# Who issues the loads, and in what order: four adapters on one core, with ScalarE issuing the later weights

## The reference

```python
# itok_B_1_2: 4 expert numbers, here 1 or 2; x: (4, 512, 512); W_down: (3, 512, 256); W_up: (3, 256, 512)
Wd = W_down[stream]
bd = b_down[stream]
Wu = W_up[stream]
bu = b_up[stream]
g = ln_w[stream]
b = ln_b[stream]
residual = hidden_states
h = jnp.einsum('bsh,bhk->bsk', hidden_states, Wd) + bd[:, None, :]
h = jax.nn.gelu(h, approximate=False)
h = jnp.einsum('bsk,bkh->bsh', h, Wu) + bu[:, None, :]
h = residual + h
mean = jnp.mean(h, axis=-1, keepdims=True)
var = jnp.mean(jnp.square(h - mean), axis=-1, keepdims=True)
h = (h - mean) * jax.lax.rsqrt(var + LN_EPS)
return h * g[:, None, :] + b[:, None, :]
```

## Time and profile before

| | |
|---|---|
| median of the runs shown | 71.18 us (72.03, 70.78, 71.18) |
| the profiled execution | 71.47 us |
| its span (first to last instruction) | 69.5 us |
| TensorE busy | 57.6 us, 83% of the span |
| VectorE, GpSimd, ScalarE busy | 48.4, 39.6, 34.5 us |
| read from device memory, written | 10.50 MB, 4.19 MB |

### The profile page before, as it was taken

How to read it: one execution, slowest core, us unless ns; L and a number is a source line. 1 busy time by engine, 2 the same in 40 slices (tenths; PEclk the granted TensorE clock), 3 DMA queues, 4 the chain that set the end, 5 groups by cost and what they waited for, 6 DMA issues and landing times. The chain is left out here.

```text
span 69.5 us, 957 instructions
## 1 busy us (share of the span) xinstructions
PE 57.6 (83%) x290; PEld 46.9 (67%) x290; DVE 48.4 (70%) x95; ACT 34.5 (50%) x51; POOL 39.6 (57%) x43
## 2 busy tenths in 40 slices
PE   1980089999999999999999999999999999993000
PEld 1960043468978888888888888888899988880000
DVE  0079510503277999964999999369999989999920
ACT  0420049257999982469996073998035404030000
POOL 4000006002939999999997599999929503029300
PEclk9999999999999999999999999999999999999995
DMA  0699998499999999999910006620000166300551
GB/s 0 217 251 271 308 421 335 71 409 306 325 417 422 419 412 414 411 408 415 379 42 0 0 5 261 257 90 0 0 9 0 73 250 280 139 12 0 194 207 51
DMA packets 4756, 14.75 MB, mean 212 GB/s; under 512 B 528, under 2 KB 528, under 8 KB 4752
## 3 DMA queue, kind: packets, MB, share of 16 engines
q1 hardware_dynamic: 4176, 13.65, 51.5%
q10 hardware_dynamic: 576, 1.05, 5.1%
HBM read 10.50 MB, written 4.19 MB: 211 GB/s over the span
## 5 line engine op out<-in xcount | busy, mean ns | idle before, releaser
L536 PE MATMUL y_ps<-wu_hi,hid_hi 128*128 128x512 f32 x32 | 13.4, 418 | 0.0
L226 POOL TENSOR_TENSOR wu_lo<-w_raw,wu_hi 128x512 fp32r<-128x512 f32 x8 | 10.2, 1288 | 5.3 <-ACT wu_hi L282 5.3
L366 DVE BATCH_NORM_STATS2 stats<-y_ps 128x6 f32<-128x512 f32 x16 | 10.8, 689 | 3.0 <-PE y_ps L542 3.0
L215 POOL TENSOR_TENSOR x_lo<-x_raw,x_hi 128x512 fp32r<-128x512 f32 x10 | 12.7, 1292 | 0.0
L542 PE MATMUL y_ps<-wu_hi,hid_lo 128*128 128x512 f32 x32 | 12.6, 394 | 0.0
L538 PE MATMUL y_ps<-wu_lo,hid_hi 128*128 128x512 f32 x32 | 12.5, 392 | 0.0
L231 POOL TENSOR_TENSOR rstd<-var_eps,minus_half 128x2 f32<-128x2 f32 (+1 forms) x10 | 6.4, 637 | 9.9 <-DVE var_eps L374 9.9
L383 DVE SCALAR_TENSOR_TENSOR y_ps<-y_ps,mean_var,ln_gb 128x512 f32<-128x512 f32 x16 | 11.5, 749 | 0.0
L393 DVE SCALAR_TENSOR_TENSOR result<-y_ps,rstd,ln_gb 128x512 f32<-128x512 f32 x15 | 10.8, 743 | 0.3
L293 ACT ACTIVATE x_res<-x_raw,w_raw 128x512 f32<-128x512 f32 x16 | 10.2, 712 | 0.0
L449 PE MATMUL hid_ps<-x_raw,w_raw 128*128 128x512 f32 x8 | 5.7, 874 | 4.0 <-DMA w_raw<-weights 4.0
(11 more groups left out here) (35 smaller groups left out, 90.6 us busy)
## 6 DMA issues: line engine op xcount, KB each, us to landing
x_raw<-x_cols SPq DMA_DIRECT2D x6, 512.0 KB, 8.3
out<-result SPq DMA_DIRECT2D x6, 512.0 KB, 3.0
w_raw<-weights SPq DMA_DIRECT2D x4, 512.0 KB, 8.3
ln_gb<-ln_rows SPq DMA_DIRECT2D x4, 512.0 KB, 12.0
w_raw<-weights SPq DMA_DIRECT2D x3, 516.0 KB, 8.8
x_raw<-x_cols ACTq DMA_DIRECT2D x4, 256.0 KB, 4.1
out<-result SPq DMA_DIRECT2D x4, 256.0 KB, 2.4
w_raw<-weights SPq DMA_DIRECT2D x1, 260.0 KB, 6.3
```

The source lines that it names most:

```text
L215: nc.gpsimd.tensor_tensor(x_lo[:, b % 2, k, :], x_raw[:, b, k, :], x_hi[:, b % 2, k, :].bitcast(F32), ALU.subtract).then_inc(x_lo_done, 1)
L226: nc.gpsimd.tensor_tensor(wu_lo[:, b % 2, j, :], raw_wu(b, j, j + 1)[:, 0, :], wu_hi[:, b % 2, j, :].bitcast(F32), ALU.subtract).then_inc( ...
L366: nc.vector.bn_stats(stats[:, b % 2, t, :], y_ps[:, t, :]).then_inc(stats_done, 1)
L536: nc.tensor.matmul(y_ps[:, t, :], hid_hi[:, p, j, rows], wu_hi[:, p, j, :], start=False, stop=False, skip_group_check=True)
```

## The change

Six edits:

- TensorE: 12 warm-up products in place of 7.
- x of batch 0 comes in two transfers of 512 KB (4 KB a partition) in place of four of 256 KB (2 KB a partition). ScalarE issues the first half; SP issues the second, behind both halves of Wd and ahead of Wu. Everything that waits for x of batch 0 waits for a half.
- ScalarE, right after its one transfer, reads the expert numbers of batches 1 to 3, and only then loads its table.
- ScalarE issues Wd and Wu of batch 1 after `residual(0)`, of batch 2 after `hi_wd(1)`, of batch 3 after `hi_wu(1)`, and the layer-norm rows of batch b after `hi_wu(b)`. Each issue takes its row from a register.
- SP no longer reads these numbers. It issues x of batch 1 and the layer-norm rows of batch 0 behind Wu of batch 0, then waits for Wu of batch 1 to land (`wu_in[1]`) before it issues x of batch 2, and for `wu_in[2]` before x of batch 3.
- GpSimd splits the second half of x of batch 1 ahead of the first half of Wd of batch 1, not behind it.

```diff
@@ constants
-WARM_UP_PRODUCTS = 7
+WARM_UP_PRODUCTS = 12
@@ SP
+            row = weights[bass.ds(expert, 1), :, :].rearrange("e q n -> (e q) n")
...
-            load_wu(0)
+            load_x(0, 1)
+            sp.dma_start(w_raw[:, 0, WU0:WROW], row[:, WU0:WROW]).then_inc(wu_in[0], DMA)
             load_x(1, 0)
             load_x(1, 1)
-            _, others = nc.values_load_multi_w_load_instructions(
-                expert_of_batch[0:1, 1:B], engines=(mybir.EngineType.SP,), min_val=0, max_val=weights.shape[0] - 1)
-            expert.extend(others)
-            for b in range(1, B):
-                if b > 1:
-                    load_x(b, 0)
-                    load_x(b, 1)
-                load_wd(b)
-                load_wu(b)
-                load_ln(b - 1)
-            load_ln(LAST)
+            sp.dma_start(ln_gb[:, 0, :, :].rearrange("q a h -> q (a h)"),
+                         ln_rows[bass.ds(expert, 1), :].to_broadcast([P, 2 * H])).then_inc(ln_in[0], DMA)
+            for b in range(2, B):
+                sp.wait_ge(wu_in[b - 1], DMA)
+                load_x(b, 0)
+                load_x(b, 1)
@@ GpSimd
-                    lo_wd(b + 1, 0)
+                    if b:
+                        lo_wd(b + 1, 0)
                     lo_x(b + 1, 2)
                     lo_x(b + 1, 3)
+                    if not b:
+                        lo_wd(b + 1, 0)
                     lo_wd(b + 1, 1)
@@ ScalarE
-            for k in range(KT):
-                act.dma_start(x_raw[:, 0, k, :], x_cols[0, :, k, :]).then_inc(first_x_in[k], DMA)
+            act.dma_start(x_raw[:, 0, 0:HALF, :], x_cols[0, :, 0:HALF, :]).then_inc(x_in[0][0], DMA)
+            _, expert = nc.values_load_multi_w_load_instructions(
+                expert_of_batch[0:1, 1:B], engines=(mybir.EngineType.Activation,), min_val=0,
+                max_val=weights.shape[0] - 1)
+
+            def load_weights(b):
+                row = weights[bass.ds(expert[b - 1], 1), :, :].rearrange("e q n -> (e q) n")
+                act.dma_start(w_raw[:, b, 0:WD_END], row[:, 0:WD_END]).then_inc(wd_in[b], DMA)
+                act.dma_start(w_raw[:, b, WU0:WROW], row[:, WU0:WROW]).then_inc(wu_in[b], DMA)
+
+            def load_ln(b):
+                act.dma_start(ln_gb[:, b, :, :].rearrange("q a h -> q (a h)"),
+                              ln_rows[bass.ds(expert[b - 1], 1), :].to_broadcast([P, 2 * H])).then_inc(ln_in[b], DMA)
...
             residual(0)
+            load_weights(1)
             gelu(0, 0)
...
             hi_wd(1)
+            load_weights(2)
             for b in range(1, B):
                 hi_wu(b)
+                if b == 1:
+                    load_weights(LAST)
+                load_ln(b)
                 residual(b)
@@ TensorE, down_whole (VectorE's split_x and ScalarE's residual likewise)
-                    pe.wait_ge(first_x_in[k], DMA)
                     if k % HALF == 0:
+                        pe.wait_ge(x_in[0][k // HALF], DMA)
                         pe.wait_ge(first_wd_in[k // HALF], DMA)
```

More of the change, by code:

```diff
@@ L88, in bias_up @@
             return w_raw[:, b, BIAS0 + JT + k:BIAS0 + JT + k + 1]
-        first_x_in = [sem(f"first_x_in{k}") for k in range(KT)]
+        x_in = [[sem(f"x_in{b}{c}") for c in range(2)] for b in range(B)]
         first_wd_in = [sem(f"first_wd_in{c}") for c in range(2)]
-        x_in = [None] + [[sem(f"x_in{b}{c}") for c in range(2)] for b in range(1, B)]
         wd_in = [first_wd_in[1]] + [sem(f"wd_in{b}") for b in range(1, B)]
@@ L153, in _ @@
         def _(sp):
-            expert = [sp.value_load(expert_of_batch[0:1, 0:1], min_val=0, max_val=weights.shape[0] - 1)]
-            def row_of(b):
-                return weights[bass.ds(expert[b], 1), :, :].rearrange("e q n -> (e q) n")
+            expert = sp.value_load(expert_of_batch[0:1, 0:1], min_val=0, max_val=weights.shape[0] - 1)
+            row = weights[bass.ds(expert, 1), :, :].rearrange("e q n -> (e q) n")
             def load_x(b, c):
@@ L161, in load_x @@
                 sp.dma_start(x_raw[:, b, ks, :], x_cols[b, :, ks, :]).then_inc(x_in[b][c], DMA)
[L163 to L171, removed]
             def store(b):
@@ L177, in store @@
                     sp.dma_start(out_rows[b, :, ts, :], result[:, b % 2, ts, :]).then_inc(stored[b][c], DMA)
-            sp.dma_start(w_raw[:, 0, 0:HALF * BN], row_of(0)[:, 0:HALF * BN]).then_inc(first_wd_in[0], DMA)
-            sp.dma_start(w_raw[:, 0, HALF * BN:WD_END], row_of(0)[:, HALF * BN:WD_END]).then_inc(first_wd_in[1], DMA)
-            load_wu(0)
+            sp.dma_start(w_raw[:, 0, 0:HALF * BN], row[:, 0:HALF * BN]).then_inc(first_wd_in[0], DMA)
+            sp.dma_start(w_raw[:, 0, HALF * BN:WD_END], row[:, HALF * BN:WD_END]).then_inc(first_wd_in[1], DMA)
+            load_x(0, 1)
+            sp.dma_start(w_raw[:, 0, WU0:WROW], row[:, WU0:WROW]).then_inc(wu_in[0], DMA)
             load_x(1, 0)
             load_x(1, 1)
-            _, others = nc.values_load_multi_w_load_instructions(
-                expert_of_batch[0:1, 1:B], engines=(mybir.EngineType.SP,), min_val=0, max_val=weights.shape[0] - 1)
-            expert.extend(others)
-            for b in range(1, B):
-                if b > 1:
-                    load_x(b, 0)
-                    load_x(b, 1)
-                load_wd(b)
-                load_wu(b)
-                load_ln(b - 1)
-            load_ln(LAST)
+            sp.dma_start(ln_gb[:, 0, :, :].rearrange("q a h -> q (a h)"),
[4 more added lines that the diff above has]
+                load_x(b, 1)
             for b in range(LAST):
@@ L288, in residual @@
                 for k in range(KT):
[L289 to L292, removed]
+                    act.wait_ge(x_in[b][k // HALF], DMA)
                     nc.scalar.activation(x_res[:, b % 2, k, :], x_raw[:, b, k, :], ACT.Identity,
@@ L345, in split_x @@
                 p, n = b % 2, KT * b + k + 1
-                dve.wait_ge(x_in[b][k // HALF] if b else first_x_in[k], DMA)
+                dve.wait_ge(x_in[b][k // HALF], DMA)
                 nc.vector.tensor_copy(x_hi[:, p, k, :], x_raw[:, b, k, :]).then_inc(early_x_hi_done, 1)
```

## The result

| | before | after |
|---|---|---|
| median | 71.0 us (70.78 to 72.03, 4 runs) | 72.44 us (71.71 to 72.67, 4 runs) |
| profiled execution | 71.47 us | 72.67 us |
| its span | 69.5 us | 70.5 us |

The ratio to the kernel before is 1.0167, with a 95% interval of 1.0096 to 1.0239: the changed kernel is 1 to 2.4% slower. The forecast was 67.2 us, and 69.3 was the top of its range. Every ratio is against the kernel before.

A forecast was written before the change was run, and what follows sets the result against it. From 8.94 us on, TensorE's queue of products was taken to bound the kernel. Starting it 4.0 us earlier, less 0.1 lost at the five issues, gave 67.2 us, range 66.1 to 69.3.

The forecast's parts named there:

- The first half of Wd, issued at 2.65 as now: Start: SP's issue of Wd stays at 2.65 us; it lands at 5.8 in place of 8.9.
- Transfers at the start: Step pricing first loads: 253 GB/s for 2 KB pieces, 412 for 4 KB, plus 2.1 us fixed.
- x's second half at 8.1: Start, behind Wd: x of batch 0's second half lands at 8.1 us, so the third product at 8.4 doesn't wait.
- Loads of the later batches: Batches 1 and 2: Wd issued at about 10 us, Wu landed by 15.3, x of batch 2 by 19.5; cost nothing.
- The warm-up: Start on TensorE: twelve products end at 6.7 us with the clock raised; down(0,1) starts at 10.1, 4.0 us earlier.
- ScalarE's register load: Ahead of ScalarE's table load: 3.2 us, read by 4.4, table loaded by 5.7, hidden by the wait for Wd; cost nothing.
- Rival A: ScalarE's register load is slow (6.5 us), TensorE loses 1.5: 68.7 us; sign: table after 7.5 us; chance 0.10.
- The five issues: On ScalarE ahead of gelu(1,0): 2.6 us, gelu(1,0) 1.3 us late, slack just used up; cost 0.1 us.
- Rival B: Issues on ScalarE are dear, 0.85 us each, TensorE loses 1.0 to 1.7: 68.5 us; chance 0.08.
- the slower case: ScalarE's issues block, at the five ahead of gelu(1,0): 1.7 us each gives 73 us; chance 0.03.
- Rival C: Clock stays low: longer warm-up doesn't raise it, or it falls in the gap behind; 69.0 us; chance 0.08.
- The sum: Whole kernel: 71.47 - 4.0 + 0.1 = 67.6 us profiled, 67.2 us against the median of 71.18.

The follow-up runs named there:

- e6: Kernel before with the first x in two halves of 4 KB pieces, both issued by ScalarE, 7 warm-up products: 70.6 us.
- e11: Changed kernel with the first x in quarters of 2 KB pieces, slices 2 and 3 by SP behind Wd: median 70.95 us, ratio 1.005.
- e12: Changed kernel, SP issuing nothing behind the first x's second half until it landed: taken up 4.9 us after issue; no total time given.
- e14: Changed kernel with first x in 2 KB quarters, x of batch 2 waiting for x of batch 1 instead of Wu: median 68.89 us, ratio 0.974.
- e9: Kernel before with 12 warm-up products in place of 7, nothing else: median 69.43 us, ratio 0.979.
- e10: Kernel before with slices 2 and 3 of the first x (2 KB pieces) by SP behind Wd, 12 warm-up products: median 69.07 us, ratio 0.976.
- e13: Changed kernel with first x in 2 KB quarters and without SP's two waits for Wu: median 69.44 us, ratio 0.982.
- e8: Changed kernel with first x all by ScalarE, batch 1 weights before residual(0), another wait for x of batch 2, VectorE's lo_hidden first: median 70.98 us.
- e2: Kernel before with only the first x in two halves (second by SP behind Wd) and 12 warm-up products: median 72.13 us, ratio 0.996.
- e4: Changed kernel without SP's two waits for Wu: median 71.41 us, ratio 0.988.
- e7: Kernel before with first x in four 2 KB quarters, slices 2 and 3 by SP behind Wd, 7 warm-up products: 69.07 us.
- e1: Changed kernel profiled a second time, no edit: 72.22 us.

## Why the prediction was wrong

- **"The first half of Wd, issued at 2.65 as now"** (Transfers at the start). Wrong: 3.83. I let SP's register load cost what it had cost beside 2 KB pieces. e6 has 4 KB pieces and no load on ScalarE and is late (4.05); e11 has the load on ScalarE and 2 KB pieces and is not (2.64). The step priced the register load of ScalarE, which cost nothing here, and not that of SP.
- **"x's second half at 8.1"**, by 412 GB/s. This is the step that failed first and most: it landed at 12.4, 4.3 us later. The 1.2 us of Wd's delay are in it; the rest is the transfer itself, 7.6 us from issue to landing, with 133 GB/s from 7 to 9 us and a last landing mark 4.1 us behind the first. I had taken 253 and 412 GB/s for the rates of 2 KB and 4 KB pieces, and they aren't: the rates after (304 for 2 KB, 133 and 400 for 4 KB) refute that reading. The Trainium skill, page DMA: Bandwidth & Descriptors, section Specifications, which I weighed and set aside, was nearer the truth: both sizes lie above its 512 B, and larger pieces brought little. In the trace after, the median packet of 2 KB took 0.086 us and one of 4 KB 0.159; by these, sixteen engines would move 381 and 412 GB/s (an estimate), and not 253 and 412. The wrong rate itself is worth only the 0.8 us between 8.9 and 8.1; what SP issues behind the transfer is worth more (e12: 2.7 us). Why it is slow with them behind it stays open.
- **"Loads of the later batches. Cost nothing each."** Wrong, and a step of its own. Wd of batch 1 went out at 12.61, not at 10, as ScalarE stands in order behind the late x; Wu landed at 20.0, not 15.3; x of batch 2 was issued at 19.98, not 15.4, and came at 27.8. Even with the start mended this wait costs 2.1 us (e11 against e14). This step is what turned a gain of nearly nothing into a loss: TensorE was still 0.16 us ahead at `down(1,0)` and 1.13 behind at `down(2,0)`. I had checked it once, for my own times, with 3 us of slack, and had not asked what each earlier delay would do to a chain of three transfers that wait for one another.
- **The warm-up** was right: 24 recorded matmuls to 6.7 forecast and 6.82 measured, then 0.43 us apart. e9 shows it as a gain by itself, 2.1%, and e10 the whole start as forecast (10.31 against 10.1).
- **ScalarE's register load** (3.2 us forecast) took from 1.2 to 5.0, and cost nothing behind the late Wd. Rival A was not the cause. Its mechanism exists, though: in e13 the table came at 8.72, past the 7.5 that was named as its sign, and TensorE lost 0.9 us.
- **The five issues** cost less than the 2.6 us charged: in the profile after, ScalarE was held by them 0.24 us, and 0.85 in e14. They aren't free everywhere: in e8 two issues ahead of `residual(0)` held it 1.11 us, as one of them took 1.12. "Should ScalarE's sequencer issue while an activation still runs" is what it does. Rival B falls, and with it the slower case, which had been pinned to these issues: slower came by a mechanism that no rival named.
- **Rival C** didn't occur in the changed kernel: the clock was at 2.4 GHz in `down_whole(0)`, behind the wait too. Its second form, a clock that falls in the gap behind the warm-up, occurred in e2 and e4 (last section).
- **The sum.** Even e10 and e14, with both faults removed, take 69.07 and 68.89 us, not 67.2: the ratios 0.976 and 0.974 are a gain of 1.7 and 1.8 us where 4.0 were forecast. In profiled executions e10's is 3.1 us (68.35 against 71.47), and there its trace accounts for it: `down(0,1)` 3.75 us earlier, the last matmul's end 3.6, the span 3.4, and 2.25 us around the span in place of 1.97. So what is gained at the start does come out at the end. That the medians differ by less than this may lie at the clock: one execution of before stood for all of them, but with seven products the eight matmuls took 5.12 us there and 6.17 in e6, while in e7 the clock was up from the first. No run settles this.

## What to carry to other kernels

An order of transfers is right only together with the time of issue of each: price a reordered load from rows in the same situation (just issued, with others going out behind it), not by a rate read where the queue had long been filled. A wait on the issuing queue makes later transfers hang on earlier ones, so ask for each what happens if the earlier is 5 us late. Here a wait for x of the batch before in place of its weights gave 2.1 us. And time the cheap edit of a bundle alone: twelve warm-up products in place of seven were worth 2.1%, while the bundle was a loss.

## What the runs showed of the hardware that I had not expected

- A register load of one number takes 0.54 us beside transfers of 2 KB pieces (e11) and 1.95 beside two of 4 KB pieces (e6), at the same time of the run and with the same pointer load (0.85 and 0.84).
- A gap can cost twice. In the profiled execution of e2 (73.0 us, where the fastest took 70.02) TensorE waited 3.63 us for x, and the clock that the warm-up had raised was down for the matmuls behind it; `down(0,1)` came 2.38 us behind the wait in place of 1.42. e4 has the same behind 3.96 us. In the changed kernel the clock was still up behind 3.52 us, and in e1 behind 3.20. The windows of TensorE in e2 (busy, clock, DMA share, GB/s):

```profile
9.00:12.40 3.40, 0.36 (x1) 1.00 0.92 352
12.60:15.80 3.20, 3.20 (x6) 0.50 0.46 157
16.00:20.00 4.00, 4.00 (x28) 1.00 0.98 319
```

- VectorE's cast and subtraction take 0.43 and 0.69 us alone and 1.1 to 1.5 and 1.7 beside GpSimd's (e8). In the changed kernel one such subtraction began 0.07 us after GpSimd's:

```profile
19.55 3.00 POOL L198 TENSOR_TENSOR x_lo<-x_raw,x_hi 128x512 fp32r<-128x512 f32 x2 [0.24 <-ACT x_hi L258]
19.62 1.78 DVE L349 TENSOR_TENSOR x_lo<-x_raw,x_hi 128x512 fp32r<-128x512 f32 x1
```

The Trainium skill, SBUF — State Buffer, section Who interferes with whom, has this as a lock on a shared pair of ports, held for a whole instruction. The trace agrees in size: 1.78 us is 0.69 and the better part of one GpSimd instruction of 1.3.
